# A mixture-of-experts kernel on one core: own slot buffers for the last two routings, five staging buffers for the second expert's chunks, tile list and slot table made at earlier steps

## The reference

```python
x = x + tanh(g_xattn) * wkv(time_decay, time_first, layernorm(x), ctx)      # scan over 256 steps
xf = layernorm(x).reshape(4096, 512)
topk_logits, sel = top_k(xf @ router, 2); cw = softmax(topk_logits)         # 8 experts
C = 1280                                                                    # places of an expert
pos = exclusive_cumsum(one_hot(sel.flatten(), 8))[.., chosen]; valid = pos < C
buf[expert, pos] = xf[token]
out_buf = (silu(gate) * up) @ w_down[e]      where gate, up = split(buf[e] @ w_up_gate[e])   # 352 wide
routed[token] += cw * out_buf[expert, pos]   # if valid
shared = (silu(xf @ s_gate) * (xf @ s_up)) @ s_down                                          # 1408 wide
out = x + tanh(g_ffn) * (routed + shared)
```

## Time and profile before

| what | us |
|---|---|
| median of three runs | 1249.8 |
| lowest and highest | 1247.11, 1252.27 |
| the profiled execution, its own time | 1249.73 |
| its span in the profile | 1248.0 |
| PE busy | 1176.1 (94%) |
| PEld, DVE, ACT, POOL busy | 829.3, 668.4, 508.3, 650.1 |

### The profile page before, as it was taken

How to read it: one execution, slowest core, us unless ns; L and a number is a source line. 1 busy time by engine, 2 the same in 40 slices (tenths; PEclk the granted TensorE clock), 3 DMA queues, 4 the chain that set the end, 5 groups by cost and what they waited for, 6 DMA issues and landing times. The chain is left out here.

```text
span 1248.0 us, 25960 instructions
## 1 busy us (share of the span) xinstructions
PE 1176.1 (94%) x8508; PEld 829.3 (66%) x8508; DVE 668.4 (54%) x1329; ACT 508.3 (41%) x915; POOL 650.1 (52%) x754
## 2 busy tenths in 40 slices
PE   1479999999999999999999897899999999999998
PEld 1367777777777777777777676466666666666653
DVE  6776776776776767767767855222222322222112
ACT  5566444443544534534435343233333333333220
POOL 7888456456456555565567641344444444444320
PEclk9999999999999999999999999899999999999999
DMA  8381122212212212212222312899899999988738
GB/s 236 88 236 44 52 60 61 58 52 59 70 40 59 76 38 55 76 51 49 87 69 39 75 35 56 181 175 189 162 178 175 170 173 173 171 164 142 122 52 317
DMA packets 177648, 136.11 MB, mean 109 GB/s; under 512 B 117789, under 2 KB 142389, under 8 KB 177440
## 3 DMA queue, kind: packets, MB, share of 16 engines
q1 hardware_dynamic: 158688, 97.55, 32.9%
q0 software_dynamic: 18048, 37.47, 17.3%
q10 hardware_dynamic: 832, 0.02, 0.0%
HBM read 69.83 MB, written 44.97 MB: 92 GB/s over the span
## 5 line engine op out<-in xcount | busy, mean ns | idle before, releaser
L1000 PE MATMUL PU<-xT,wreg 128*128 128x256 f16 x4224 | 507.2, 275 | 5.1 <-DVE srng L1280 5.1
L1000 PEld LDWEIGHTS PU<-xT,wreg 128*128 128x128 f16 x4224 | 413.9, 99 | 78.4 <-DVE srng L1280 4.8
L734 POOL DMA_INDIRECT moe_d<-wkv,acc x71 | 112.0, 1578 | 218.6 <-ACT wkv L904 212.9
L1106 PE MATMUL PU<-acc,wkv 128*128 x1284 | 217.0, 315 | 4.3 <-DMA wkv<-xT 4.3
L1033 PE MATMUL PD<-wreg,hreg 128*128 128x512 f16 x858 | 206.4, 379 | 0.0
L1106 PEld LDWEIGHTS PU<-acc,wkv 128*128 128x128 f16 x1284 | 126.1, 98 | 75.3 <-issue 4.8
L815 ACT ACTIVATE srng<-PU 128x256 f32<-128x256 f32 x176 | 67.2, 382 | 263.4 <-PE PU L1000 233.7
L615 POOL TENSOR_TENSOR hreg<-srng,hreg 128x256 f16<-128x256 f32 x165 | 123.5, 751 | 65.7 <-ACT hreg L831 64.4
L1127 PE MATMUL PD<-acc,wkv 128*128 (+1 forms) x639 | 149.6, 379 | 1.5 <-DVE wkv L1505 1.5
L1505 DVE TENSOR_TENSOR wkv<-PR,wkv 128x384 f16<-128x384 f32 x71 | 39.6, 558 | 208.0 <-ACT wkv L898 208.0
L1033 PEld LDWEIGHTS PD<-wreg,hreg 128*128 128x128 f16 x858 | 84.0, 98 | 73.5
(11 more groups left out here) (176 smaller groups left out, 1364.9 us busy)
## 6 DMA issues: line engine op xcount, KB each, us to landing
wreg<-in_L_ffn_w_up_gate SPq DMA_DIRECT2D x48, 176.0 KB, 4.0
acc<-in_x SPq DMA_DIRECT2D x32, 256.0 KB, 3.0
wkv<-in_ctx SPq DMA_DIRECT2D x32, 256.0 KB, 2.7
xhl_d<-wkv SPq DMA_DIRECT2D x32, 256.0 KB, 2.2
moe_d<-acc SPq DMA_DIRECT2D x13, 512.0 KB, 3.8
out<-moe_d SPq DMA_DIRECT2D x2, 3328.0 KB, 21.2
acc<-n_L_ffn_shared_w_up_gate SPq DMA_DIRECT2D x16, 256.0 KB, 5.9
wreg<-in_L_ffn_w_down SPq DMA_DIRECT2D x12, 256.0 KB, 4.3
```

Source lines behind the costliest of these rows:

```text
L734: pool.indirect_dma_start(out=moe_d, out_offset=bass.IndirectOffsetOnAxis(ap=didx[:, t:t + 1], axis=0), in_=ostage[t % 3], in_offset=None, ...
L1000: mm = pe.matmul(PU[r][:, gu * UN:(gu + 1) * UN], sU[:, m, gu, a, kt, :], xT[:, u.par, b, kt, :], start=(kt == 0 and a + b == 0), stop=(kt ...
L1106: mm = pe.matmul(up_set[t % 2][gu][:, 0:I], xgT[:, t % 4, a, kt, :], weights(h, ((gu * 2 + b) * KT + kt) * I, P, I), start=(kt == 0 and a ...
```

## The change

It has four parts. (1) A routing gets a place `at` in `sidx` and `stw`: 0 for all but the last, which has 2. The last routing writes the second half of both, and its wait on `slots_sent` asks only for the sends of tiles 0 to 27, as the wait of the routing before it does. (2) The chunks of expert 1 go through five staging buffers (`SECOND`), three of them new in freed rows of `acc`. They are converted at the steps of `SECOND_AT`, from 2 to 9, in places two in a step. SP waits once for the held sums in DRAM (`moe_started`) before them, and the first four row transposes no longer stand behind SP's wait for the end of unit 15's up products. (3) The tile list is made sooner: `count_all` in step 3, `place_tiles` in step 4, `place_homes` in step 5, `place_experts` in step 6; `place_drains` moves back to step 10. (4) The slot table is turned ahead of `up_pair` of step 9, and `slot_indices` stands in DVE's step 9.

```diff
+SECOND = 5
+TABLE_AT = 9
+SECOND_AT = {2: [0], 3: [1, 2], 4: [3], 5: [4], 6: [5, 6], 7: [7], 8: [8, 9], 9: [10]}
...
+LAST = [Route(GROUPS - 1, 14 * (GROUPS - 1), TILES - GT, UT, 0), Route(GROUPS, 14 * (GROUPS - 1) + 12, TILES - UT, UT, UT)]
...
+        wst += wst + [freed(D) for _ in range(SECOND - 2)]
...
-                if e < EARLY and w >= 2:
+                if e == 0 and w >= 2:
                     sp.wait_ge(ew_lo, w - 1)
+                elif e == 1:
+                    sp.wait_ge(ew_lo, max(WCH, w - SECOND + 1))
...
+            sp.wait_ge(moe_started, 16 * MOE_PARTS)
             for q in range(WCH):
                 load_chunk(1, q)
-            sp.wait_ge(up_ready, JT * UNITS)
             for t in range(4):
                 turn_slots(t)
+            sp.wait_ge(up_ready, JT * UNITS)
...
-            unit(Unit(0, UNITS - 1), 0, lambda q: weights_hi(1, q))
+            def second_hi(m):
+                for q in SECOND_AT.get(m, ()):
+                    weights_hi(1, q)
+            unit(Unit(0, UNITS - 1), 0, second_hi)
...
-                            if u.v == UNITS - 1 and s == 4:
+                            if u.v == UNITS - 1 and s == 3:
                                 count_all()
-                            if u.v == UNITS - 1 and s == 8:
+                            if u.v == UNITS - 1 and s == 5:
                                 place_homes()
...
-                        if u.fixed and u.v == UNITS - 1 and s == JT - 1:
+                        if u.fixed and u.v == UNITS - 1 and s == TABLE_AT:
                             turn_table()
...
-                    wait_alone(slots_sent, 16 * TOPK * r.c0)
+                    wait_alone(slots_sent, 16 * TOPK * (r.c0 - lo))
...
-                        if u.v == UNITS - 1 and s == 5:
+                        if u.v == UNITS - 1 and s == 4:
                             place_tiles()
-                        if u.v == UNITS - 1 and s == 7:
+                        if u.v == UNITS - 1 and s == 10:
                             place_drains()
+                        if u.v == UNITS - 1 and s == 6:
+                            place_experts()
                         if u.v == UNITS - 1 and s == 9:
-                            place_experts()
+                            slot_indices()
...
-            slot_indices()
```

More of the change, by code:

```diff
@@ L107, in tile @@
         return UT * self.v + k
-class Route(namedtuple("Route", "i base c0 nt")):
+class Route(namedtuple("Route", "i base c0 nt at")):
     @property
@@ L253, in build @@
         assert fr[0] <= HOMES * EW // 2
+        wst += wst + [freed(D) for _ in range(SECOND - 2)]
+        assert fr[0] <= HOMES * EW // 2
         sUw = wreg[:, 0:JT * 2048].bitcast(F32)
@@ L332, in chunk_home @@
         def chunk_home(w):
+            if w < WCH:
+                return w % 2, 16 * (w // 2 + 1)
             if w < EARLY * WCH:
-                return w % 2, 16 * (w // 2 + 1)
+                n = w - WCH
+                return 2 + n % SECOND, 16 * (n // SECOND + 1)
             n = w - EARLY * WCH
-            return 2 + n % STAGED, 16 * (n // STAGED + 1)
+            return 2 + SECOND + n % STAGED, 16 * (n // STAGED + 1)
         def chunks_at(t):
@@ L344, in chunks_at @@
             return [(n + EARLY, q) for q in range(WCH) if (q // 2 if q < 6 else q - 3) == m]
-        ew_in = [sem(f"ew_in{r}") for r in range(2 + STAGED)]
+        ew_in = [sem(f"ew_in{r}") for r in range(2 + SECOND + STAGED)]
         ew_hi = sem("ew_hi"); ew_lo = sem("ew_lo")
@@ L599, in send_slots @@
                     pool.indirect_dma_start(
-                        out=slot_d, out_offset=bass.IndirectOffsetOnAxis(ap=sidx[:, 2 * t + k:2 * t + k + 1], axis=0),
-                        in_=stw[:, k, t, :], in_offset=None).then_inc(slots_sent, 16)
+                        out=slot_d, out_offset=bass.IndirectOffsetOnAxis(ap=sidx[:, 2 * (r.at + t) + k:2 * (r.at + t) + k + 1], axis=0),
+                        in_=stw[:, k, r.at + t, :], in_offset=None).then_inc(slots_sent, 16)
             def split_up_lo(m):
@@ L1007, in turn_table @@
                 pe.wait_ge(v_used, TILES)
-                pe.wait_ge(psteps, PSTEPS + 4)
+                pe.wait_ge(psteps, PSTEPS + 2)
                 pe.matmul(PR[:, 0:NPOS], tokt[:, :, 0], Pm, start=True, stop=False)
@@ L1318, in place_drains @@
             def place_drains():
-                pstep(9, dve.tensor_tensor(begins, places[0:1].unsqueeze(2).to_broadcast([1, NPOS, E]),
+                pstep(12, dve.tensor_tensor(begins, places[0:1].unsqueeze(2).to_broadcast([1, NPOS, E]),
                                            counts[0:1, 1 + E:1 + 2 * E].unsqueeze(1).to_broadcast([1, NPOS, E]), ALU.is_equal))
-                pstep(10, dve.tensor_reduce(begin, begins, AX.X, ALU.max))
+                pstep(13, dve.tensor_reduce(begin, begins, AX.X, ALU.max))
                 dve.scalar_tensor_tensor(out=drains, in0=begin, scalar=16.0, in1=landed[:, 1:1 + NPOS],
@@ L1326, in place_experts @@
                 dve.wait_ge(homes_turned, 2)
[L1327 to L1329 removed]
+                pstep(9, dve.tensor_scalar(spare, PL[0:1, E + NPOS:E + 2 * NPOS], 1.0, -1.0, ALU.subtract, ALU.mult))
+                pstep(10, dve.tensor_tensor(spare_at, spare, spare_rows[:, 0:NPOS], ALU.mult))
+                pstep(11, dve.scalar_tensor_tensor(out=no_home, in0=PL[0:1, E + NPOS:E + 2 * NPOS], scalar=1.0, in1=no_home,
                                                   op0=ALU.subtract, op1=ALU.mult))
@@ L1376, in address_slots @@
             def address_slots(r):
-                nt, pre = r.nt, r.pre
+                nt, pre, lo = r.nt, r.pre, r.at
                 rows = rowid[:, bass.ds(r.c0, nt)]
                 if not (isinstance(r.i, int) and r.i == 0):
-                    wait_alone(slots_sent, 16 * TOPK * r.c0)
+                    wait_alone(slots_sent, 16 * TOPK * (r.c0 - lo))
                 for k in range(TOPK):
-                    dve.tensor_copy(stw[:, k, 0:nt, 0], rows).then_inc(tr_steps, 1)
+                    dve.tensor_copy(stw[:, k, lo:lo + nt, 0], rows).then_inc(tr_steps, 1)
                     dve.tensor_scalar(trash[:, k, 0:nt], rows, float(TRASH + NTOK * (k + 1)), None, ALU.add).then_inc(tr_steps, 1)
@@ L1393, in address_slots @@
                 tstep(r, 10, dve.tensor_tensor(sl, sl, tr, ALU.add))
-                step(r, pre + 8, dve.tensor_copy(sidx[:, 0:2 * nt].rearrange("p (t n) -> p n t", n=2), sl))
+                step(r, pre + 8, dve.tensor_copy(sidx[:, 2 * lo:2 * (lo + nt)].rearrange("p (t n) -> p n t", n=2), sl))
             def route_slots(r):
@@ L1488, in _, with second_lo @@
                 unit(Unit(0, v), 0, lambda m: early_lo(v, m))
-            unit(Unit(0, UNITS - 1), 0, lambda q: weights_lo(1, q))
+            def second_lo(m):
+                for q in SECOND_AT.get(m, ()):
+                    weights_lo(1, q)
+            unit(Unit(0, UNITS - 1), 0, second_lo)
             end = Unit(0, UNITS - 1)
-            slot_indices()
             hidden(end, JT - 1)
```

7 lines of the change are left out of this document (3 added, 4 removed).

## The result

| | before | changed |
|---|---|---|
| median of the runs, us | 1248.97 (6 runs) | 1237.51 (6 runs) |
| lowest and highest, us | 1247.11, 1252.27 | 1234.04, 1241.0 |
| profiled execution, its own time | 1249.73 | 1241.0 |
| its span | 1248.0 | 1239.2 |

The ratio is 0.9904 with a 95% interval of 0.9882 to 0.9927: the change takes 11.5 us off the median (0.92% by the medians, 0.96% by the ratio). The forecast was a time of 1236.4, 13.3 us under the 1249.73 it started from.

A forecast was written before the change was run, and what follows sets the result against it. PE bounds the expert phase, so gains lie in its waits and half clock around unit 15. Starting experts 10.7 us earlier plus 2.6 from full clock makes 13.3, from 1249.73 to 1236.4 us; range 1233 to 1241.

The forecast's parts named there:

- The bound: Expert phase: PE busy every microsecond at full clock, 5.85 us a tile; gains lie only in unit 15 and behind it.
- The sum: Unit 15 to first expert tiles: 10.7 us earlier start plus 2.6 from full clock, 13.3 in all, giving 1236.4.
- the distance: From unit 15's first up_pair product to the first expert product; PE forecast ready for the experts at 778.2.
- the first tiles: Start of the expert phase: without idle time ahead it runs at full clock, winning 2.6 us.
- The wait at the homes: New PE wait ahead of place_homes in step 5 for the end of place_tiles, 2.2 us, possibly nothing or 4.
- The rows: Transposed rows for the first expert product, there at 777.3, 0.9 us before PE is ready at 778.2.
- the clock behind the new wait: Unit 15 after place_homes: fall priced at zero, about 1.7 us if it comes; as rival 1238 to 1240, chance 0.12.
- the 2.27 us wait of the kernel before: PE's wait before pair 4 in unit 15, clock stayed 1.00 after it; taken as the nearer likeness for the new wait.
- the two late `hidden` of the middle steps: Unit 15: they stood behind chunks waiting for loads; with five staging buffers this wait costs nothing.
- The gather chain: Rival, indices to first transposed rows: 2 to 4 us longer than reckoned, 1237.5 to 1242; chance 0.17.
- given back in the expert phase: Rival: waits for gathers or scatters appear there with DMA at 0.95 busy, 1244 to 1250; chance 0.07.
- the slower case: Rival: half clock from the new wait in step 5 until the experts run, 1255.7; chance 0.04.

The follow-up runs named there:

- e0: The changed kernel run again with no edit; median 1235.59 us, ratio to the kernel before 0.9896.
- e9: The changed kernel run a third time with no edit; median 1237.4 us, ratio to the kernel before 0.9909.
- e5: The kernel before with part 1 alone, plus the new order of SP's and the transposes' waits; median 1244.13 us, ratio 0.9977.
- e6: The kernel before with parts 1 and 2 alone, plus the new order of SP's and the transposes' waits; median 1237.06 us, ratio 0.9911.
- e3: The changed kernel with part 2 undone (two staging buffers, one chunk a step) but for SP's waits; median 1238.07 us, ratio 0.9919.
- e7: The changed kernel with place_homes and place_experts one step later and two staging buffers, one chunk a step; median 1232.03 us, ratio 0.9872.
- e4: The changed kernel with part 4 undone: table turned at step 10, slot_indices after DVE's last step; median 1240.55 us, ratio 0.9941.
- e2: The changed kernel with part 1 undone: last routing writes the first half of the slot buffers again; median 1240.17 us, ratio 0.9923.
- e1: The changed kernel with place_homes in step 6 and place_experts in step 7, each one step later; median 1233.95 us, ratio 0.9887.

## Why the prediction was right

**The bound.** It stood as read. The expert phase is as long as it was, at 36 x 200 / 1233 = 5.84 us a tile, and the gain, 11.5 us in the first profile and 13.2 in e0, comes out of the stretch from unit 15 to the first expert tile.

**The sum, where the clock did not fall.** The forecast for the distance was 778.2 - 737.97 = 40.2, and e0 shows 40.26; for the first tiles it had 2.6 us won, measured were 2.5. The wait at the homes was forecast at 2.2 and came as 2.44, because the list ended 0.2 later than reckoned. No wait was forecast before pair 4, at the table and before the experts, and none came. The rows were there 1.7 us ahead of PE (1.9 in e0), where I had 0.9: from the end of the indices to the rows it took 780.97 - 772.73 = 8.2 us, not the 9.25 taken over from before.

**The step that failed: the clock behind the new wait.** I took the 2.27 us wait of the kernel before, which left the clock at 1.00, as the nearest row, priced the fall at zero, and gave it a chance of 0.12. In two of three profiles of the changed kernel the clock fell, and it cost 41.94 - 40.26 = 1.7 us, the price that the prediction had named for it. The median of 1237.51 lies between 1236.4 and the 1238.1 with a fall, but the spread of the runs is too wide to read from it how often the clock fell. That the time came out within 1.1 us is in part luck: 11.5 us were gained and not 13.3, and 0.8 of the difference was made up by the kernel before, whose median was now 1248.97 and not 1249.73. The Trainium skill says that what the gate looks at runs free of the kernel, so that one program can lose different amounts (TensorE: Matmul & The Clock Gate, Part 1). The trace agrees: e0 and e9 are one kernel, with waits of 2.43 and 2.44, and show both outcomes.

**The gain, booked in part to the wrong parts.** I had the two late `hidden` of the middle steps, 0.66 and 1.06, down to the staging buffers. The 0.66 went with part 1 alone (e5); the 1.06 stayed there and went with the five buffers (e6), so that one was booked rightly. With the list and the table at their new steps part 2 gives only 0.1 to 0.6 us (e3, e7), while it gives 6.1 at the old ones (e6). Parts 2 and 4 remove the same hindrance of the rows by two ways: either takes the last chunk from ahead of the indices. So the parts don't add up: undone one at a time parts 1, 2 and 4 cost 3.9, 0.1 and 2.3 us, and of the last up to 1.9 are `place_drains`, which part 3 had put there; part 1 alone, added to the kernel before, gives 1.5 of distance. No run undoes part 3 alone in the changed kernel. Added to parts 1 and 2 it gives 0.8 us (e4 beside e6, no fall at the homes), less than the 1.7 that a fall costs. Parts 3 and 4 together give 1.5 us of distance over e6 with the fall and 3.1 without, which the medians (1237.06 for e6) don't show. With the homes one step later it is 5.6.

**The other rivals.** The gather chain did not end last; nothing was given back in the expert phase, since what is gained from unit 15 to the first tiles is still there at the end of the span (11.6 and 13.2 us); the low clock, where it came, was over within 8 us of the wait, so the slower case had no ground.

## What to carry to other kernels

When work is moved earlier for an engine that waits, look up on the other engine when its input is ready, and place the wait behind that: one step too early cost this change 2.4 us every time and 1.7 more in some executions. Measure from a fixed product before the change to a fixed product behind it, rather than by the span; the start of the kernel moved the spans by more than most of these edits. Several edits that free the same wait don't add up (the five buffers gave 6.1 us without parts 3 and 4 and 0.1 to 0.6 with them), so undo each one alone and also add each one alone before giving it a price.

## What the runs showed of the hardware

A wait of PE of 2.4 us in the middle of dense matmuls can leave the clock alone or bring it down: in the five profiles with a wait of 2.43 to 2.58 us ahead of the homes the granted clock fell in three, and stayed at 1.00 in two. A wait of 2.68 before pair 4 (e2) left it at 1.00, one of 3.50 at the homes of the same profile did not. Where it fell, to the lower of its two levels (1.2 GHz instead of 2.4), it cost 1.6 to 1.7 us and was back at 1.00 within 8 us. The kernel alone doesn't decide it: of three profiles of the same kernel two show the fall. Ahead of the thin products of the table turn (71 columns) a wait of 2.36 (before, e5) or 2.13 (e6) was followed by the low clock in all three profiles, at a price of 1.7 us in the first and 3.2 in the other two; one of 2.15 ahead of the experts' full products (e4) was not.

The sends to the slot table took a varying time to land. POOL waited between 4.04 us (e9) and 5.42 us (e1) for them ahead of the table load, against 4.20 before. The number of staging buffers doesn't explain it: with two it was 4.20 (before) to 5.22 us (e7), with five it was 4.04 to 5.42. This had cover each time, and I have not tried what it depends on.
